# The prologue of a three-stage decoder layer, written out as an order of its own

## The reference

```python
x = layernorm(x + mixer(x))             # in_w, causal conv of 4 taps, silu, xp_w, scan over 16 states, out_w
x = layernorm(x + cross_attention(ctx_1024, x))   # layernormed inputs, 8 heads of 128, Wq, Wkv, Wo
x = layernorm(x + moe(x))               # top-2 of 8 experts of inner width 512, capacity 512 tokens
```

## Time and profile before

| | |
|---|---|
| median of 3 runs | 1116.28 us (1115.92 to 1116.43) |
| the profiled execution, own time | 1119.2 us |
| its span in the profile | 1117.2 us |
| TensorE busy | 1006.8 us, 90% of the span |
| VectorE busy | 801.6 us, 72% |
| ScalarE busy | 664.0 us, 59% |
| GpSimd busy | 514.8 us, 46% |
| mean granted TensorE clock | 0.953 of full speed |

### The profile page before, as it was taken

The page is one execution under the profiler, slowest core; times in us unless marked ns, Lnnn a source line. Parts: engine busy times, 40 slices in busy tenths (PEclk is TensorE's granted clock), DMA queues, the critical chain, the costliest instruction groups (busy, mean ns, idle before and its releaser), DMA issues.

```text
span 1117.2 us, 20866 instructions
## 1 busy us (share of the span) xinstructions
PE 1006.8 (90%) x6878; PEld 939.0 (84%) x6878; DVE 801.6 (72%) x2021; ACT 664.0 (59%) x1713; POOL 514.8 (46%) x826
## 2 busy tenths in 40 slices
PE   2479999999999999999999999999999999389970
PEld 1368999999999999999999999999999898279960
DVE  2557777788778877887788778777887776245436
ACT  2347666666666666666667666757675655045535
POOL 1422436373537353645364446544554543324653
PEclk7689999999999999999999999999999999679995
DMA  9340212020302030103010301030103000475548
GB/s 308 91 167 23 72 30 97 18 72 21 101 23 67 17 111 25 56 17 114 22 55 16 114 22 56 16 114 22 56 16 105 22 32 11 160 241 82 80 51 302
DMA packets 60365, 84.46 MB, mean 76 GB/s; under 512 B 13940, under 2 KB 43688, under 8 KB 60264
## 3 DMA queue, kind: packets, MB, share of 16 engines
q1 hardware_dynamic: 52584, 70.46, 19.1%
q0 software_dynamic: 7680, 12.72, 5.6%
HBM read 44.16 MB, written 38.99 MB: 74 GB/s over the span
## 4 chain that ended last, share of the span: by engine, by line
PE 76%; ACT 9%; DVE 6%; issue 3%; DMA 3%; POOL 2%; SPq 1%; ACTq 0%; DVEq 0%; POOLq 0%
PE ps L546 21%; PE ps L548 20%; PE ps L547 20%; PE ps L573 6%; PE ps L631 3%; PE ps L639 3%; DVE nmx L1302 2%; ACT prob L919 2%; PE ps L679 1%; ACT fx L999 1%; ACT k_hi L808 1%; ACT pT_hi L934 1%; DMA slots<-xrow,slot_u 1%; ACT x2T L862 1%; DMA oww<-in_out_w 1%
## 5 line engine op out<-in xcount | busy, mean ns | idle before, releaser
L1478 POOL TENSOR_SCALAR prob<-prob,rinv 128x333 f32<-128x333 f32 x256 | 140.7, 561 | 354.8 <-DVE rinv L1311 354.2
L914 ACT ACTIVATE oT_hi<-ps 128x256 fp32r<-128x256 f32 x128 | 49.2, 385 | 196.3 <-PE ps L548 196.3
L546 PE MATMUL ps<-kv_lo,w_hi 128*128 128x256 f32 (+1 forms) x512 | 159.0, 310 | 4.8 <-DVE vst_lo L1007 1.9
L548 PE MATMUL ps<-kv_hi,w_hi 128*128 128x256 f32 (+1 forms) x512 | 153.6, 300 | 0.0
L547 PE MATMUL ps<-kv_hi,w_lo 128*128 128x256 f32 (+1 forms) x512 | 153.3, 299 | 0.0
L919 ACT ACTIVATE prob<-ps,nmx 128x333 f32<-128x333 f32 x256 | 135.0, 537 | 8.8 <-DVE nmx L1302 8.1
L1007 DVE TENSOR_TENSOR pT_lo<-ps,pT_hi 128x512 fp32r<-128x512 f32 (+1 forms) x256 | 130.2, 550 | 0.6 <-ACT pT_hi L934 0.6
L1302 DVE TENSOR_REDUCE nmx<-ps 128x2 f32<-128x666 f32 x128 | 108.7, 849 | 22.2 <-PE ps L548 21.1
L573 PE MATMUL ps<-ident,prob 128*128 128x128 f32 (+1 forms) x768 | 108.0, 273 | 3.4 <-DVE oT_lo L1007 2.7
L546 PE MATMUL ps<-pT_lo,v_hi 128*128 128x256 f32 (+1 forms) x384 | 108.4, 282 | 0.9 <-DVE pT_lo L1007 0.9
L548 PE MATMUL ps<-pT_hi,v_hi 128*128 128x256 f32 (+1 forms) x384 | 108.3, 282 | 0.0
(11 more groups left out here) (223 smaller groups left out, 3008.7 us busy)
## 6 DMA issues: line engine op xcount, KB each, us to landing
wraw<-in_W SPq DMA_DIRECT2D x14, 512.0 KB, 6.7
vcd_hi<-vst_hi SPq DMA_DIRECT2D x10, 512.0 KB, 2.7
vcd_lo<-vst_lo SPq DMA_DIRECT2D x10, 512.0 KB, 3.6
v_hi<-vcd_hi SPq DMA_DIRECT2D x32, 154.0 KB
v_lo<-vcd_lo SPq DMA_DIRECT2D x32, 154.0 KB
slots<-initr SPq DMA_DIRECT2D x8, 520.0 KB, 8.5
xts<-in_xT SPq DMA_DIRECT2D x16, 256.0 KB, 3.9
xs<-in_x SPq DMA_DIRECT2D x16, 256.0 KB, 3.9
```

The lines of the kernel that those rows point to most:

```text
L546: pe.matmul(dst, hi1, lo2, start=first, stop=False, skip_group_check=True)
L548: return pe.matmul(dst, hi1, hi2, start=False, stop=last, skip_group_check=True)
L914: act.activation(oT_hi[:, h % 2, :], ps[:, AVB, 0:S], ACT.Copy).then_inc(oTh_set, 1)
L1478: pool.tensor_scalar(prob[:, h % 2, t, 0:KEYS], prob[:, h % 2, t, 0:KEYS], rinv[:, h % 2, t:t + 1], 1.0, ALU.mult, ALU.mult).then_inc(norm ...
```

## The change

Passes -2 and -1 are dropped from `bodies`. Each engine gets a function `first()` instead that issues the same work in an order written by hand:

- Weight chunks 0 and 1 are now Wv, 2 and 3 Wk. SyncE asks for them in another order between the small loads; `cxs` and `xpr` come earlier, `xs` later.
- The input of batch 1 is loaded at once into `full`, a buffer that is free at that time, with a semaphore of its own (`xT1_ld`).
- Units of the prologue take any of the eight PSUM banks, idle ones too.
- The two context tiles and the eight products of the folded bias stand in other places of the order. The second lo half of tile 1's `vc` and `v`'s lo half are done in slot 0 of batch 0 (`first_value`).
- `w_lo` of chunks 2, 3, 6 and 7 is made by GpSimd (`tensor_tensor`, semaphore `wk_lo_set`), of chunks 0, 1, 4 and 5 by VectorE as before.
- ScalarE runs a small Exp on `warm` first.
- VectorE waits for `oww` only after the taps of batch 0.
- The clearing of `slots` and `accd` is issued by SyncE at the end of `first()`, and GpSimd fills `initr` after the first context tile's normalisation.

```diff
-            body(-2, 0, {"aft"}, set(), 0)
-            body(-1, 1, {"aft", "nxt", "ctx", "more"}, {"aft"}, 0)
...
@@ SyncE @@
+            def first():
+                sp.dma_start(xts[:], xT_d[0]).then_inc(xT_ld, 16)
+                sp.dma_start(inw[:], in_w).then_inc(inw_ld, 16)
+                sp.dma_start(vec[:], vecs).then_inc(vec_ld, 16)
+                sp.dma_start(cxs[:], ctxt[0]).then_inc(ctx_ld, 16)
+                sp.dma_start(xpr[:], xp_w).then_inc(xpr_ld, 16)
+                sp.dma_start(full[:], xT_d[1]).then_inc(xT1_ld, 16)
+                load_parts(range(0, 2))
...
+                load_parts(range(2, 4))
+                sp.wait_ge(owx_set, 1)
+                for row in (0, 32, 64):
+                    sp.dma_start(oww[row:row + NST + 1, :], out_w).then_inc(oww_ld, 16)
+                next_context(1)
+                load_parts(range(4, 6))
+                sp.dma_start(xs[:], x_d[0]).then_inc(x_ld, 16)
+                load_parts(range(6, 8))
+                keep_context(0)
...
+                keep_values(0)
+                sp.wait_ge(vc_st, 32)
+                sp.wait_ge(wk_lo_set, 2)
+                sp.wait_ge(w_lo_set, 4)
+                values(0, 0)
+                next_context(2)
+                keep_context(1)
+                keep_values(1)
+                sp.wait_ge(initr_set, 2)
+                for e in range(E):
+                    sp.dma_start(slots[e * CAP:(e + 1) * CAP, :].rearrange("(s p) c -> p s c", p=P),
+                                 initr[:]).then_inc(init_st, 16)
...
@@ TensorE, waits left out @@
+            def first():
+                unit("in", 0, 0, 0, ps[:, 5, :])
+                unit("in", 1, 0, 0, ps[:, 7, :])
+                unit("cT", 0, 0, 0, ps[:, 6, :])
+                unit("in", 0, 1, 0, ps[:, 0, :], full)
+                unit("in", 1, 1, 0, ps[:, 1, :], full)
+                unit("xp", 0, 0, 0, ps[:, 2, :])
+                unit("vc", 0, 0, 0, ps[:, 0, :])
+                unit("vc", 1, 0, 0, ps[:, 4, :])
+                unit("cT", 0, 1, 0, ps[:, 6, :])
+                value_bias(range(0, 3))
+                unit("op", 0, 0, 0, ps[:, 5, :])
+                value_bias(range(3, H))
...
+                unit("ln", 0, 0, 0, ps[:, 6, :])
+                unit("vc", 0, 1, 0, ps[:, 2, :])
+                unit("k", 0, 0, 0, ps[:, 7, :])
+                unit("q", 0, 0, 0, ps[:, 5, :])
+                unit("vc", 1, 1, 0, ps[:, 4, :])
+                unit("v", 0, 0, 0, ps[:, 7, :])
...
@@ ScalarE @@
+            def first():
+                act.wait_ge(const_set, 1)
+                act.activation(warm[:], powm[:], ACT.Exp)
+                act.wait_ge(bq_set, 1)
+                act.wait_ge(zero_set, 1)
+                for u in range(2):
+                    unit("in", u, 0, 0, ps[:, 5 + 2 * u, :])
+                    first_tap(0, u)
+                unit("cT", 0, 0, 0, ps[:, 6, :])
+                split_hi([0])
+                tanh_half(-1, 0)
+                split_hi([1])
+                tanh_half(-1, 1)
+                split_hi([2, 3])
+                unit("in", 0, 1, 0, ps[:, 0, :])
+                act.wait_ge(small_ld, 48)
+                unit("xp", 0, 0, 0, ps[:, 2, :])
+                unit("in", 1, 1, 0, ps[:, 1, :])
+                state_hi(-1)
+                unit("vc", 0, 0, 0, ps[:, 0, :])
+                unit("vc", 1, 0, 0, ps[:, 4, :])
+                unit("cT", 0, 1, 0, ps[:, 6, :])
+                split_hi([4, 5])
+                first_tap(1, 0)
+                first_tap(1, 1)
+                unit("ln", 0, 0, 0, ps[:, 6, :])
+                split_hi([6])
+                unit("vc", 0, 1, 0, ps[:, 2, :])
+                unit("k", 0, 0, 0, ps[:, 7, :])
+                split_hi([7])
+                unit("q", 0, 0, 0, ps[:, 5, :])
+                unit("vc", 1, 1, 0, ps[:, 4, :])
+                unit("v", 0, 0, 0, ps[:, 7, :])
...
@@ VectorE, after its memsets @@
+            def first():
+                context_stats(0)
...
+                for u in range(2):
+                    for k in range(1, TAPS):
+                        tap(0, 2 * u, k)
+                        tap(0, 2 * u + 1, k)
+                silu(0, 0)
+                context_hi(0)
+                context_stats(1)
+                silu(0, 1)
+                split_lo([0, 1])
+                dve.wait_ge(oww_ld, 48)
...
+                unit("xp", 0, 0, 0, ps[:, 2, :])
+                scan(-1, 1, 0)
+                state_lo(-1, 1)
+                unit("vc", 0, 0, 0, ps[:, 0, :])
+                mixed(-1, 1, 0, ps[:, 5, :])
+                unit("vc", 1, 0, 0, ps[:, 4, :])
+                context_hi(1)
+                latents(-1, 1, 0)
+                split_lo([4])
...
+                latents_hi(-1, 1, 0)
+                split_lo([5])
+                unit("k", 0, 0, 0, ps[:, 7, :])
+                unit("vc", 0, 1, 0, ps[:, 2, :])
+                unit("q", 0, 0, 0, ps[:, 5, :])
+                for k in range(1, TAPS):
+                    tap(1, 0, k)
+                    tap(1, 1, k)
...
             STEPS_AT = {
-                (0, "N"): [t_(2, 1)],
+                (0, "N"): [("att", first_value), t_(2, 1)],
...
@@ GpSimd @@
+            def first():
+                pool.wait_ge(const_set, 1)
+                context_norm(0)
...
+                pool.memset(initr[:], 0.0).then_inc(initr_set, 1)
...
+                context_lo(0)
+                context_norm(1)
+                split_lo([2, 3])
+                powers(0)
+                context_lo(1)
+                latents_part(-1, 1)
+                normalised(-1, 1)
+                split_lo([6, 7])
```

More of the change, by code:

```diff
@@ L407, in _, with load_parts @@
         def _(sp):
[L408 to L430, removed]
+            def load_parts(chunks):
+                for c in chunks:
+                    src = CHUNKS[c][0]
+                    dst = staged(c)
+                    if len(src.shape) == 3:
+                        dst = dst.rearrange("p (h n) -> p h n", n=D)
+                    sp.dma_start(dst, src).then_inc(part_ld[c], 16)
             def expert_weights(experts, group):
@@ L598, in project, with unit @@
                 last.then_inc(wo_mm, 1)
-            def unit(name, idx, bb, par, g):
+            def unit(name, idx, bb, par, g, rows=xts):
                 if name in "kqv":
@@ L899, in tanh_half, with split_hi, state_hi @@
                                scale=0.5).then_inc(th_set, 1)
-            act.wait_ge(bq_set, 1)
-            act.wait_ge(small_ld, 48)
-            act.wait_ge(zero_set, 1)
+            def split_hi(chunks):
+                for c in chunks:
+                    _, which, half = CHUNKS[c]
+                    act.wait_ge(part_ld[c], 16)
+                    act.activation(w_hi[:, which, 1024 * half:1024 * (half + 1)], staged(c),
+                                   ACT.Copy, scale=1.0 if which else QSCALE).then_inc(w_hi_set, 1)
+            def state_hi(b):
+                need(act, ys_set, b + 2)
+                need(act, op_mm, b + 1)
+                for row in (0, 64):
+                    act.activation(ys_x[row:row + NST, :], ys[:], ACT.Copy).then_inc(ysh_set, 1)
+            def first():
[31 more added lines that the diff above has]
+                unit("v", 0, 0, 0, ps[:, 7, :])
+            first()
             def body(b, par, have, had, tile):
@@ L947, in body @@
                         second_weight(b - 1)
-                    for c in HI_AT[h] if at(b, -1) else ():
-                        _, which, half = CHUNKS[c]
-                        act.wait_ge(part_ld[c], 16)
-                        act.activation(w_hi[:, which, 1024 * half:1024 * (half + 1)], staged(c),
-                                       ACT.Copy, scale=1.0 if which else QSCALE).then_inc(w_hi_set, 1)
                     if at(b, B - 1) and h == 0:
@@ L1251, in u_, with split_lo @@
                 return "aft", lambda b, par, tile: tap(b + 2, ct, k)
+            def split_lo(chunks):
+                for c in chunks:
+                    _, which, half = CHUNKS[c]
+                    o = (slice(None), which, slice(1024 * half, 1024 * (half + 1)))
+                    dve.wait_ge(w_hi_set, c + 1)
+                    dve.scalar_tensor_tensor(out=w_lo[o], in0=staged(c), scalar=1.0 if which else QSCALE,
+                                             in1=ap(w_hi[o]), op0=ALU.mult, op1=ALU.subtract).then_inc(w_lo_set, 1)
@@ L1273, in _ @@
                 (6, "C"): [("nxt", latents_hi), u_(1, 1), u_(0, 2)],
-                (6, "D"): [("more", lambda b, par, tile: context_hi(tile + 1))],
                 (7, "N"): [u_(1, 2)],
@@ L1279, in _ @@
             }
-            def split_lo(chunks):
-                for c in chunks:
-                    _, which, half = CHUNKS[c]
-                    o = (slice(None), which, slice(1024 * half, 1024 * (half + 1)))
-                    dve.wait_ge(w_hi_set, c + 1)
```

(14 more changed lines are left out.)

231 lines of the change are left out of this document (118 added, 113 removed).

## The result

| | before | after |
|---|---|---|
| median, four runs each | 1116.36 us (1115.92 to 1117.41) | 1091.43 us (1090.87 to 1091.78) |
| the profiled execution, own time | 1119.2 us | 1091.12 us |
| its span | 1117.2 us | 1089.4 us |
| mean granted TensorE clock | 0.953 | 0.964 |

The ratio is 0.9775, with an interval from 0.9758 to 0.9792: faster, by 24.9 us. I had forecast 1081.1 us, in a range from 1076.5 to 1089.0; the result lies 2.4 us above the range. The mark, the start of batch 0's second scores, moved from 81.70 to 52.01 us, by 29.7 and not by 35.2.

What follows compares the result with a forecast made beforehand. TensorE bounds the loop over 16 batches; the change shortens only the prologue. Gains of 19.6, 0.8 and 15.5 less a loss of 0.7 make 35.2 us, taking the median from 1116.28 to 1081.1, range 1076.5 to 1089.

Steps and rivals of the forecast that it cites:

- the contention term: Time added where VectorE works beside GpSimd's w_lo parts: 1.0 us for gt, scan and state_lo, 1.3 for batch 1's taps.
- stretch B: Second SiLU half to the start of xa: 10.0 us before, 9.2 after, a gain of 0.8.
- A: Prologue to the end of the second SiLU half: 37.5 us before, 17.9 after, a gain of 19.6.
- C: Start of xa to the end of the first q_lo: 26.7 us before, 11.2 after, a gain of 15.5.
- D: First q_lo to batch 0's second scores: 7.5 us before, 8.1 after, a loss of 0.6 to 0.8.
- the `vcd` store: Before the first q_lo: SyncE's store and its landing, 4.7 us, hold vst_hi in the binding path of 11.2 us.
- the branch over `lnp`, `ln`, `full` and `kv_lo`: From xa to q: estimated at 8.9 us, hidden by 2 us under the path through the store.
- the tap of 834 ns: Profile row of a VectorE tap beside GpSimd, 834 ns against 479; read as slowing by less than a whole instruction.
- GpSimd's parts hold VectorE up: Rival, 19 in 100: VectorE instructions with two SBUF inputs wait out GpSimd's 2.5 us parts; 4.4 us less gain, 1085.5.
- the signs that I named for being wrong: GpSimd parts over 4 us each, taps beside them over 1 us, ScalarE waiting beyond 35 us, or batch 2 waiting for xts.
- The clearing's cover: Moved table writes on SyncE's queue: xts of batch 2 lands by 66.5 us, wanted at 68.1, so no cost.
- Only the oww hole closes: Rival, 7 in 100: some order taken as hidden binds and 26.7 us of the prologue stay; gain 19.7, 1096.6 us.

Runs made afterwards that it cites:

- wk_fix: Changed kernel with w_lo chunk 2 moved to VectorE ahead of xp and chunk 3 on GpSimd behind state_lo; 1096.29 us, ratio 0.9736 to the kernel before.
- wo_lo_memset: Changed kernel with GpSimd's subtractions for w_lo chunks 6 and 7 replaced by memsets to zero; 1092.63 us, ratio 0.9719 to the kernel before.
- best2: Changed kernel with w_lo chunks 2, 3, 6 and 7 re-placed, GpSimd's chunk 6 waiting for VectorE's chunk 5; 1089.67 us, ratio 0.9687 to the kernel before.
- oww_only: Kernel before with only the wait for oww and the five instructions behind it moved later; 1119.02 us, ratio 0.9949.
- after_c: Changed kernel unaltered, run again as reference in the third group; 1096.45 us, ratio 0.9757 to the kernel before.
- best: Changed kernel with w_lo chunks 2, 3, 6 and 7 re-placed, chunk 6 without a wait for VectorE's chunk 5; 1093.28 us, ratio 0.9717 to the kernel before.
- after_again: Changed kernel unaltered, run again as reference in the second group; 1095.78 us, ratio 0.9738 to the kernel before.

## Why the prediction was wrong

The mechanism and the size of most steps held; the failed step is the contention term, which I priced by "0.35 for four taps, 1.3", and with 1.0 in stretch B. The holds cost 7.0 us (2.7 and 4.3) where I had 2.3, and these 4.7 us are most of the 5.5 that are missing at the mark. By stretches, in the profiled executions:

| stretch | forecast | measured | |
|---|---|---|---|
| A, to the end of the second SiLU half | ends 17.9 | 17.2 | 0.7 better |
| B, to the start of `xa` | 9.2 | 11.0 | 1.8 worse |
| C, to the end of the first `q_lo` | 11.2 | 12.4 | 1.2 worse |
| D, to the mark | 8.1 | 11.4 | 3.3 worse |

**A** held in all: taps at 10.15 (10.3 said), no wait for `oww`, `cxn` done at 9.1 (9.5), no wait for tile 1's load.

**B.** `xp` began at 17.40 and took 2.83 us, between my bounds for it. Against 0.41 and 0.68 us unhindered, `gt` and scan lost 2.7 us where I took 1.0. With their neighbour moved (wk_fix) they lost nothing. The rival had this at "3 us in place of 1.0". The rest of B evens out: `xp` took 0.8 us less than the 3.7 in my sum, and a `vst_lo` that I had not counted stood in front of `xa` for 0.6.

**C.** I took the `vcd` store as what binds, and the branch over `lnp`, `ln`, `full` and `kv_lo` as "covered by 2 us". It was the other way round: `vst_hi` of tile 1 waited for no store. From `xa`, `ln` ran only at 32.60, `full` came at 33.73, `k` at 36.20 and `q_lo` ended at 40.63. My 8.9 us of estimates for that branch were 3.5 us short: `lnp` took 1.13 for 0.7, `ln` 1.09 for 0.6, the two kv halves 1.2 for 0.9, and from there over k's and q's products and their evictions to `q_lo` it was 4.7 where I had 2.7. Since the store's branch was put at 11.2, only 1.2 of this shows.

**D.** The six taps took 6.73 us, 4.3 more than unhindered, against the 1.3 that I took; my upper bound was 3.7. The rest is `v`: I let TensorE's work hide under VectorE's, but `v` waits for `v_lo` behind `nmx` and then ran at the lower clock level: `k_lo` was done at 51.30, and the second scores behind `v` began 0.7 us later. wo_lo_memset takes the first away and the mark comes at 46.92, 0.4 beside my 46.5. That nearness is luck in part: there `q_lo` ends at 40.47 and not at 38.3, and D takes 6.4 us and not 8.1. best2 repairs both halves and it comes at 45.42.

**The row that I misread.** The price came from the tap of 834 ns, which I called "less than a whole instruction". The timelines of GpSimd and of VectorE in the kernel before show what lay beside it:

```profile
64.26 0.72 POOL L1458 TENSOR_TENSOR cx_lo<-cfull,cx_hi 128x256 fp32r<-128x256 f32 x1 [8.14 <-DVE cx_hi L1126]
...
64.43 0.83 DVE L1065 SCALAR_TENSOR_TENSOR cv<-hp,vec,cv 128x256 f32<-128x256 f32 x1
```

GpSimd's `cx_lo` was itself only 0.72 us long. The tap began 0.17 us into it, at 64.43, waited to its end at 64.98, and ran: 0.55 of waiting in 0.83. It did wait out the whole instruction; that instruction was short. Next to one of 2.5 us the same rule gives 2.6, as measured. A rise by 0.35 us is no property of a tap but of its neighbour. The Trainium skill, page "SBUF — State Buffer", section "Who interferes with whom", says just this, that the loser waits for the whole instruction; the runs agree with it (2.63 us beside 2.65), and so did the row that I held against it.

The row held more. The two taps behind that one, of 0.48 and 0.61 us, began under GpSimd's next instruction, `x<-xa`, which has one full-size input, and did not wait out its 1.63 us. The timelines of GpSimd and VectorE in the kernel after show the same with longer instructions:

```profile
35.65 2.45 POOL L1587 TENSOR_SCALAR x<-xa,a_mv,a_rs 128x256 f32<-128x256 f32 x1
35.87 1.21 DVE L1316 SCALAR_TENSOR_TENSOR w_lo<-staging,w_hi 128x1024 fp32r<-128x1024 f32 x1
```

`w_lo` began second and took its usual 1.21 us; it was GpSimd's instruction that took 2.45, where the next of its kind took 1.22. `cxn` with its 4.57 us is such a case too: VectorE's w_lo parts beside it, 2.35 us for two, were no longer than usual, and it ended 1.0 us behind them. The section speaks of any GpSimd instruction that reads SBUF. In these runs only those with two full-size inputs held VectorE up.

**The rival.** "GpSimd's parts hold VectorE up" had 19 in 100 and 1085.5 us, and it is what happened; "in D the taps stop until 42 (3.7 in place of 1.3)" was short of the 4.3 since GpSimd began part 6 at 40.63, not at 37: the normalised x and the addition of `cvec`, 3.66 and 1.29 us, stood before it. Of the signs that I named for being wrong one came: taps beside the parts took over 1 us. The parts themselves took 2.4 to 2.7 us, near my 2.5.

**Behind the mark.** Of the 10.3 us between forecast and result, 5.5 lie ahead of the mark (35.2 - 29.7), some 1.6 behind it, nearly all of them in one place, and 3.2 in how I went from one execution to the median. The maxima of the loop's heads run about 30.1 us ahead of the kernel before from the third head to slot 4 of batch 14 (846.36 against 876.42 us). One slot later it is 28.6. The stretches of 1 us there, in the kernel after and in the kernel before (busy PE, PEld, DVE, ACT, POOL with counts, granted clock, DMA share, GB/s):

```profile
849.00:850.00 1.00, 0.00 (x0) 0.00 (x0) 0.41 (x2) 0.97 (x3) 1.00 (x2) 1.00 0.03 8
850.00:851.00 1.00, 0.52 (x3) 0.31 (x3) 1.00 (x3) 0.93 (x3) 0.00 (x0) 1.00 0.00 0
851.00:852.00 1.00, 1.00 (x5) 1.00 (x6) 0.96 (x3) 0.00 (x0) 0.00 (x0) 0.56 0.00 0
852.00:853.00 1.00, 1.00 (x7) 1.00 (x7) 0.96 (x6) 0.00 (x0) 0.00 (x0) 0.50 0.00 0
853.00:854.00 1.00, 1.00 (x6) 1.00 (x6) 0.11 (x2) 0.15 (x1) 0.81 (x1) 0.50 0.00 0
854.00:855.00 1.00, 1.00 (x8) 1.00 (x7) 0.28 (x1) 0.69 (x2) 0.24 (x1) 0.73 0.00 0
```

```profile
879.00:880.00 1.00, 0.00 (x0) 0.00 (x0) 0.41 (x2) 0.97 (x3) 1.00 (x2) 1.00 0.00 0
880.00:881.00 1.00, 0.51 (x2) 0.30 (x2) 1.00 (x3) 0.98 (x3) 0.05 (x1) 1.00 0.00 0
881.00:882.00 1.00, 0.97 (x8) 0.97 (x9) 0.97 (x3) 0.00 (x0) 0.00 (x0) 1.00 0.00 0
```

TensorE stands still for 1.6 us in both at this place (busy 0.00 in one stretch and 0.52 or 0.51 in the next). The clock stays at 1.00 before; after, it falls to 0.50 for over 3 us, and 1.5 us go. In what TensorE did ahead of it the rows show no difference. The same fall is in five of the eleven other traces (oww_only, after_c, best, best2, wk_fix), where the time from this head's maximum to the next is 9.5 us as here, in place of 8.0. It is not in the other six, among them after_again, the same kernel; TensorE's pause at this place is 1.6 to 1.7 us in all thirteen. So it is no effect of the change that I can show, and a kernel can have it in one execution and not in another.

**The median.** I took the profiled execution (1119.2 us) to be 2.9 above the median for both kernels, and subtracted the gain from the median. The changed kernel's profiled execution took 1091.12 us, 0.3 below its median. Gained were 28.1 us between the profiled executions, 24.9 between the medians. On the other two chips that ran the changed kernel again the medians gained 29.3 and 26.4. What made that one execution of the kernel before longer, or its medians shorter, stays open: no trace of the others exists.

**What held besides.** The clearing's cover (writes from 49.5 to 61.4, no wait in the in unit of batch 2), the weight order at no cost, the second input buffer, the idle banks. The clearing's cover was added up 1 us too tight: 43.7, 13.3 and 8.5 make 65.5 and not 66.5. "Only the oww hole closes" priced the hole at 19.7 us; that edit alone gives 5.2, since two loads then stand behind the clearing.

## What to carry to other kernels

Before an elementwise step goes to another engine to relieve the first, list what the first engine runs at that very time, and whether both read two full-size inputs from SBUF: then each instruction caught costs what is left of the neighbour's length, not its own share. Put the step beside instructions that read one of their inputs from PSUM, or where the other engine waits anyway, and make it wait there explicitly; in best2 one such wait turned 3.38 us into 1.21. And a slowdown read from one row is a price only when the neighbour's own length stands beside it.

## What the hardware showed that was not expected

- A held instruction shows as a long one, not as idle time: 16 x 256 elements in 2.45 us instead of 0.41. No view of waits lists it.
- Instructions with one input in PSUM were not held beside the same GpSimd subtraction (`v_lo` 0.68 us, `nmx` 0.84).
- A GpSimd instruction with one full-size input did not hold VectorE's: it lost itself (2.45 us in place of 1.22), though it had begun first.
- The same 1.6 us of idle TensorE in the same code dropped the granted clock to 0.50 in six traces and left it at 1.00 in seven.
- Two chips can agree on a prologue of 82 us within 0.1 us and differ by 7.6 us over 16 batches of the same code, with a mean granted clock of 0.953 on both.
